# Deformable weights turned among the first products, and half an image out of PSUM before the second convolution: one fused network block on one core

## What is computed

```python
x = x + deformable(_gn(x))          # _gn: 32 groups of 4 channels
x = x + residual_block(_gn(x))

# deformable: om = conv3x3(x, w_off) gives 27 channels: 9 y-offsets, 9 x-offsets, 9 masks;
#   every tap samples x bilinearly at its own fractional position, times sigmoid(mask);
#   out = einsum(samples, weight) + bias, then a norm over 16 groups, gamma, beta
# residual_block: q = ternary(w) in {-1, 0, 1}
#   out1 = relu(batchnorm(conv3x3(x, q1)))
#   out2 = batchnorm(conv3x3(out1, q2));  return relu(out1 + out2)
```

## Time and profile before

| what | us |
|---|---|
| median of 3 runs (291.68 to 292.33) | 292.24 |
| the profiled execution, whole | 290.57 |
| its span, first to last instruction | 288.8 |
| TensorE busy | 251.1 |
| VectorE busy | 193.7 |
| ScalarE busy | 170.6 |
| GpSimd busy | 137.6 |

### The profile page before, as it was taken

How to read it: one execution, slowest core, us unless ns; L and a number is a source line. 1 busy time by engine, 2 the same in 40 slices (tenths; PEclk the granted TensorE clock), 3 DMA queues, 4 the chain that set the end, 5 groups by cost and what they waited for, 6 DMA issues and landing times.

```text
span 288.8 us, 5556 instructions
## 1 busy us (share of the span) xinstructions
PE 251.1 (87%) x1980; PEld 217.0 (75%) x1980; DVE 193.7 (67%) x450; ACT 170.6 (59%) x365; POOL 137.6 (48%) x193
## 2 busy tenths in 40 slices
PE   2699898999899899989989999999899949999900
PEld 2567567899898899989988889988687727777700
DVE  5588736989888996779977899770466253115194
ACT  2568646989669878878998778840143033330061
POOL 9202899967659688857769975140000000000040
PEclk9999997999999999999999999999999997999965
DMA  7915676543433323333323333000000000000016
GB/s 201 390 30 182 210 256 233 158 124 135 138 129 114 122 61 115 120 96 114 97 85 100 128 123 101 25 2 0 0 0 2 0 0 0 0 3 0 5 38 257
DMA packets 25737, 28.13 MB, mean 97 GB/s; under 512 B 2525, under 2 KB 23629, under 8 KB 25704
## 3 DMA queue, kind: packets, MB, share of 16 engines
q1 hardware_dynamic: 25200, 26.47, 28.1%
q10 hardware_dynamic: 504, 1.24, 1.2%
HBM read 19.87 MB, written 6.78 MB: 92 GB/s over the span
## 4 chain that ended last, share of the span: by engine, by line
PE 66%; DVE 16%; ACT 7%; DMA 4%; issue 2%; POOL 2%; SPq 1%; ACTq 0%; POOLq 0%
PE PS L787 25%; PE PS L707 6%; PE PS L660 5%; PE PS L708 5%; PE PS L709 5%; PE PS L689 4%; PE PS L691 4%; PE PS L690 4%; DVE slo L1298 4%; DMA wd_raw<-in_L_conv_weight 3%; ACT vhi L959 3%; PE PS L594 2%; DVE vlo L1309 2%; DVE xb L1401 2%; ACT shi L947 1%
## 5 line engine op out<-in xcount | busy, mean ns | idle before, releaser
L502 POOL TENSOR_TENSOR vt<-rowm,hat 128x1026 f32<-128x1026 f32 x36 | 70.8, 1968 | 28.4 <-PE PS L669 27.2
L1309 DVE TENSOR_TENSOR vlo<-PS,vhi 128x576 fp32r<-128x576 f32 (+2 forms) x88 | 50.0, 589 | 17.0 <-ACT vhi L959 16.7
L959 ACT ACTIVATE vhi<-PS 128x576 fp32r<-128x576 f32 (+2 forms) x88 | 43.8, 524 | 17.9 <-PE PS L691 17.8
L1298 DVE TENSOR_TENSOR slo<-PS,shi 114x512 fp32r<-114x512 f32 (+1 forms) x68 | 43.2, 675 | 8.9 <-ACT shi L947 8.6
L707 PE MATMUL PS<-vhi,wdhi 128*128 128x256 f32 x144 | 43.7, 304 | 1.8 <-ACT xb L966 1.8
L527 POOL TENSOR_TENSOR xb<-xb,xs 128x512 f32<-128x512 f32 x3 | 3.7, 1280 | 86.5 <-ACT xb L1031 86.5
L689 PE MATMUL PS<-shi,patch 114*128 114x288 f32 (+1 forms) x136 | 43.5, 320 | 0.3 <-DVE vlo L1309 0.2
L787 PE MATMUL PS<-xhi,q 128*128 128x512 f32 (+1 forms) x144 | 38.7, 415 | 4.2 <-ACT xhi L1026 4.2
L691 PE MATMUL PS<-shi,patch 114*128 114x288 f32 (+1 forms) x136 | 41.0, 301 | 0.0
L690 PE MATMUL PS<-slo,patch 114*128 114x288 f32 (+1 forms) x136 | 40.8, 300 | 0.0
L708 PE MATMUL PS<-vlo,wdhi 128*128 128x256 f32 x144 | 40.5, 281 | 0.0
(11 more groups left out here) (155 smaller groups left out, 429.6 us busy)
## 6 DMA issues: line engine op xcount, KB each, us to landing
patch<-xt SPq DMA_DIRECT2D x136, 114.0 KB
xt<-xtt SPq DMA_DIRECT2D x4, 1024.0 KB, 6.1
xs<-in_x SPq DMA_DIRECT2D x3, 512.0 KB, 8.6
out<-xb SPq DMA_DIRECT2D x6, 256.0 KB, 2.3
wraw<-in_L_conv_w SPq DMA_DIRECT2D x2, 576.0 KB, 10.8
wd_raw<-in_L_conv_weight ACTq DMA_DIRECT2D x1, 576.0 KB, 8.3
xs<-in_x SPq DMA_DIRECT2D x2, 256.0 KB, 3.7
omr<-omr SPq DMA_DIRECT2D x8, 64.0 KB, 3.8
```

Of the source, the lines that this page charges most:

```text
L502: g.tensor_tensor(vt[:, n % 2, :, :].rearrange("p t (r j) -> p t r j", r=WR), rowm[:, n % 2, :, :].unsqueeze(3).to_broadcast([P, TAPS, WR, ...
L959: last = a.activation(places(vhi), src, ACT.Copy)
L1298: d.tensor_tensor(lo, src, hi, ALU.subtract).then_inc(slo_ok, 1 if pairs(n) == 2 else 3)
L1309: last = d.tensor_tensor(places(vlo), src, places(vhi), ALU.subtract)
```

## The change

1. TensorE turns the deformable weights after the first six products, not before them, with `group_square` of image 1 between the second and third group of three; ScalarE writes `whole(GN0, 0)` ahead of the first copy of weights; VectorE's `deformable_lo(0)` goes behind the statistics of image 2.
2. GpSimd's low parts of image 2 go to VectorE (ahead of `whole_late(3)`), and VectorE's of image 3 to GpSimd, behind `distances(1)`. The four folds of the first ternary weight, which stood there, are spread over the rounds n = -1 to 1; those of the second go to n = 2 to 4.
3. Slot -1 on TensorE and ScalarE is ahead of the last three products of the offsets (3, 1) and of `tail(7)`.
4. In the first convolution the two tiny products of `GN8` of image 3 move behind the next quarter image each; VectorE takes the second half's statistics ahead of `variance(GN1, 2)`.
5. ScalarE copies PSUM bank 0 to `raw` (in `vt`, free by then) during the first convolution. Statistics, `r1` and `xhi` of half image 0 read `raw`; ScalarE writes `xhi` of half 0 first; the second convolution starts on it alone, and its seventh product waits for the second half.

```diff
+            FOLDED = {-1: ((0, 0),), 0: ((0, 1), (0, 2)), 1: ((0, 3),), 2: ((1, 0),), 3: ((1, 1),), 4: ((1, 2), (1, 3))}
...
                 if n == -4:
-                    for level in range(FOLDS):
-                        fold_weights(0, level)
-                if 0 <= n < FOLDS:
-                    fold_weights(1, n)
+                    low_parts(3)
+                for i, level in FOLDED.get(n, ()):
+                    fold_weights(i, level)
...
-            for part in range(2):
-                for h in range(2):
-                    offset_part(0, h, part)
+            offset_part(0, 0, 0)
+            for m in range(2):
+                turn_deformable(m)
+            group_square(GN0, 1)
+            turn_deformable(2)
+            offset_part(0, 1, 0)
+            for h in range(2):
+                offset_part(0, h, 1)
...
-                pe.wait_ge(ready, (B, 2)[part] + b + 1 if done is c1_mm else 2 * b + h + 1 + (h == 0))
+                if done is c1_mm:
+                    pe.wait_ge(ready, (B, 2)[part] + b + 1)
+                else:
+                    pe.wait_ge(ready, 2 * b + h + 1 + (h == 0 and (b, part) != (0, 0)))
                 for i, k in enumerate(TAP_ORDER[part]):
+                    if done is c2_mm and (b, h, part, k) == (0, 0, 0, 2 * K):
+
+                        pe.wait_ge(r1hi_ok, 2)
...
                 between = {(0, 0): [(group_mean, GN1, B - 2)],
-                           (0, 1): [(group_square, GN1, B - 2), (group_mean, GN8, B - 1)],
-                           (0, 2): [(group_square, GN8, B - 1)],
+                           (0, 1): [(group_square, GN1, B - 2)],
+                           (0, 2): [(group_mean, GN8, B - 1)],
+                           (1, 0): [(group_square, GN8, B - 1)],
...
+                            if (sums, n) == (group_mean, GN8):
+
+                                pe.wait_ge(gn_var, order(GN1, B - 2) + 1)
...
             turn_offsets(2)
-            offset_conv(3, 1)
+            offset_part(3, 1, 0)
             slot(-1)
+            offset_part(3, 1, 1)
...
+                act.wait_ge(c1_mm, 1)
+                act.wait_ge(vt_ok, CHUNKS)
+                a.activation(raw, PS[:, 0, :], ACT.Copy).then_inc(raw_ok, 1)
                 root(BN1, 0)
                 act.wait_ge(gn_ok, order(BN1, 0) + 1)
-                for n, hi in [(1, 1), (0, 1), (1, 0)] + [(n, hi) for n in range(2, 2 * B) for hi in (1, 0)]:
-                    if (n, hi) == (0, 1):
-                        act.wait_ge(r1_first, 1)
+                act.wait_ge(raw_ok, 1)
+                for n, hi in [(0, 1), (1, 1), (1, 0)] + [(n, hi) for n in range(2, 2 * B) for hi in (1, 0)]:
...
             heads(GN0, 0)
+            whole(GN0, 0)
             deformable_hi(0)
-            whole(GN0, 0)
...
-                variance(GN1, B - 2)
                 dve.wait_ge(y_done, 1)
                 image_stats(GN8, B - 1, halves=(1,))
+                variance(GN1, B - 2)
...
-                d.tensor_scalar(chunk(r1, 0), PS[:, 0, :], scale_of(BN1, 0), shift_of(BN1, 0), ALU.mult, ALU.add).then_inc(r1_first, 1)
+                d.tensor_scalar(chunk(r1, 0), raw, scale_of(BN1, 0), shift_of(BN1, 0), ALU.mult, ALU.add).then_inc(r1_first, 1)
...
             image_stats(GN0, 1)
-            deformable_lo(0)
             deviation(GN0, 1)
             dve.wait_ge(x_in[2], 16)
             image_stats(GN0, 2, last=False)
+            deformable_lo(0)
...
             pixels_lo(1)
+            tails(GN0, 2)
             whole_late(3)
             largest(0)
-            tails(GN0, 3)
```

More of the change, by code:

```diff
@@ L146, in build @@
         r1 = sb("r1", [P, B, HW])
+        raw = vt[:, 0, :, :].rearrange("p t q -> p (t q)")[:, 0:BIG]
         PS = ctx.enter_context(nc.psum_tensor("PS", [P, 2 * B, BIG], F32))
@@ L196, in build @@
         c1_mm, c2_mm = sem("c1_mm"), sem("c2_mm")
-        r1_first, r1_ok, r1hi_ok, r1lo_ok = (sem(n) for n in ("r1_first", "r1_ok", "r1hi_ok", "r1lo_ok"))
+        raw_ok, r1_first, r1_ok, r1hi_ok, r1lo_ok = (sem(n) for n in ("raw_ok", "r1_first", "r1_ok", "r1hi_ok", "r1lo_ok"))
         f_scaled, f_relu, out_done = (sem(n) for n in ("f_scaled", "f_relu", "out_done"))
@@ L472, in _ @@
             low_parts(0)
-            low_parts(2)
             def distances(n):
@@ L559, in _ @@
             group_square(GN0, 0)
-            for m in range(K):
-                turn_deformable(m)
             def turn_image(b):
@@ L1017, in finish @@
                 whole(GN1, B - 1)
+                act.wait_ge(c1_mm, 1)
+                act.wait_ge(vt_ok, CHUNKS)
+                a.activation(raw, PS[:, 0, :], ACT.Copy).then_inc(raw_ok, 1)
                 root(BN1, 0)
                 act.wait_ge(gn_ok, order(BN1, 0) + 1)
-                for n, hi in [(1, 1), (0, 1), (1, 0)] + [(n, hi) for n in range(2, 2 * B) for hi in (1, 0)]:
-                    if (n, hi) == (0, 1):
-                        act.wait_ge(r1_first, 1)
+                act.wait_ge(raw_ok, 1)
+                for n, hi in [(0, 1), (1, 1), (1, 0)] + [(n, hi) for n in range(2, 2 * B) for hi in (1, 0)]:
                     if hi and n // 2 >= RING:
                         act.wait_ge(c2_mm, 2 * (n // 2 - RING) + 2)
-                    dst, src, done = ((chunk(r1, n), PS[:, n, :], r1_ok), (chunk_rows(xhi, n), square(PS[:, n, :]), r1hi_ok))[hi]
+                    dst, src, done = ((chunk(r1, n), PS[:, n, :], r1_ok), (chunk_rows(xhi, n), square(PS[:, n, :] if n else raw), r1hi_ok))[hi]
                     a.activation(dst, src, ACT.Relu, bias=shift_of(BN1, 0), scale=scale_of(BN1, 0)).then_inc(done, 1)
@@ L1069, in _ @@
             slot(-2)
+            slot(-1)
             tail(7)
-            slot(-1)
             masks(2)
@@ L1215, in tails @@
                 dve.wait_ge(xhi_ok, (B if n == GN1 else 0) + b + 1)
-                dve.wait_ge(xn_late, b - 1) if (n, b) == (GN0, B - 1) else dve.wait_ge(xn_ok, (2 if n == GN1 else 0) + b + 1)
+                dve.wait_ge(xn_late, b - 1) if (n, b) == (GN0, 2) else dve.wait_ge(xn_ok, (2 if n == GN1 else 0) + b + 1)
                 d.tensor_tensor(inner(xlo, b), square(plain(b)), inner(xhi, b), ALU.subtract).then_inc(xlo_ok, 1)
@@ L1376, in conv_stats @@
                     for m in range(2 * B):
-                        dve.wait_ge(done, m + 1)
-                        ins = d.bn_stats(st[:, n, m, :], PS[:, m, :])
+                        dve.wait_ge(*((raw_ok, 1) if (n, m) == (BN1, 0) else (done, m + 1)))
+                        ins = d.bn_stats(st[:, n, m, :], raw if (n, m) == (BN1, 0) else PS[:, m, :])
                     link(ins)
```

10 lines of the change are left out of this document (5 added, 5 removed).

## The result

| | before | changed |
|---|---|---|
| median, us | 292.28 (291.68 to 294.35, 4 runs) | 288.59 (288.2 to 288.8, 4 runs) |
| the profiled execution, whole / span | 290.57 / 288.8 | 288.8 / 287.0 |

The ratio is 0.9895, 95% interval 0.9853 to 0.9938: faster by about 1%, and the median is inside the predicted range of 288.1 to 291.2. (Ratios in this document are estimates of their own, each with its interval; they are not the quotient of the two medians printed beside them.) Two differences don't agree, though: the medians are 3.7 us apart, the profiled executions 1.8. The forecast was 2.3.

A forecast was written before the change was run, and what follows sets the result against it. The prediction took TensorE, two thirds of the chain of waits, to bound the kernel. Its terms, -1.75 + 0.3 - 0.83 = -2.3 us, took the median from 292.24 to 289.9 us, range 288.1 to 291.2.

The forecast's parts named there:

- Weights among products: Opening: products start before the deformable weights are turned, bringing the replicating DMA earlier; -0.5 us, bounds 0 and -1.15.
- The rival that L1149 comes first: Opening: VectorE's small step runs ahead of GpSimd's subtraction, square 0.65 us earlier; 289.3 us, chance 0.13.
- GpSimd's folds, -1.1: Opening: one subtraction of 2.19 us replaces four folds of 3.27 ahead of the first `vt`; -1.1 us, bounds 0 and -1.1.
- Slot -1, -0.15: Slot -1: no wait for `tail(7)` first, pairs follow at once; -0.15 us, bounds +0.2 and -0.5.
- The opening together: Sum of the three opening terms, -0.5 - 1.1 - 0.15 = -1.75 us.
- First convolution, +0.3: First convolution: wait at the `GN8` mean reappears as 1.45 us at image 3's `GN1` mean; +0.3 us.
- rival bound -1.4: First convolution: lower bound, if the chain from square to aggregate is shorter by 1.4 us.
- Between the convolutions, -0.83: Between the convolutions: one ScalarE copy suffices before the second starts; -0.8 us, -0.83 in the sum, bounds -0.85 and -0.5.
- The rival that the clock holds here: Second convolution: the shorter TensorE wait of 3.4 us keeps the clock up, saving 1.6 us; 288.3 us, chance 0.10.
- From the sum to the median: Whole kernel: the gain of 2.3 us in the profiled execution is taken off the median 292.24, giving 289.9 us.
- The slower rival: First convolution: the new 1.45 us wait lets the clock fall, 291.5 us, or 293.1 with two lengths; slower, chance 0.04.

The follow-up runs named there:

- e7: Changed kernel with part 1 undone, the nine turned blocks ahead of the products again; 289.41 us, ratio 0.9891.
- e10: The kernel before, unedited, run once more for its trace; one execution, 295.93 us.
- e9: The kernel before with part 2 of the change alone; 290.76 us, ratio 0.998.
- e2: Changed kernel with parts 4 and 5 undone, only parts 1 to 3 kept; 288.96 us, ratio 0.9896.
- e3: Changed kernel with part 4 undone; 288.46 us, ratio 0.9887.
- e12: Changed kernel with `GN8` mean after a quarter's third product, GpSimd's first low parts after VectorE's deviation, image 3's low parts before `distances(0)`; 287.35 us, ratio 0.9865.
- e8: Changed kernel with GpSimd's low parts of image 0 waiting for VectorE's deviation of image 1; 288.54 us, ratio 0.9896.
- e6: Changed kernel with the four folds of the first ternary weight back ahead of the first `vt`; 294.47 us, ratio 1.0091.
- e5: Changed kernel with part 3 undone, last offset products and `tail(7)` ahead of slot -1 again; 289.27 us, ratio 0.9929.
- e1: The changed kernel again, no edit; 288.92 us, ratio 0.9907.
- e11: Changed kernel with `GN8` mean after a quarter's third product, square after that quarter, GpSimd's first low parts waiting for VectorE's deviation; 287.56 us, ratio 0.9866.

## Why the prediction was right, and where it was off

It was right in sign and range, and for the terms behind the opening nearly to the digit. By its steps:

- **Weights among products.** First product 10.28 (10.34 forecast), the held-up step to 14.25 (14.4), the square at 14.57 (14.47). Of the 0.5, the first distances show 0.31 (30.96 to 30.65), half of it the input's. What failed is the price of the turned blocks, 0.13 each: they ran at half speed, the six ahead of the square took 1.48 us and made it start 0.3 behind the end of L1167, and the three behind it took 0.68 instead of 0.4. More important, the term was sized for an execution whose wait was short. In e7 and e10 the old order stands 1.6 us before the square, and the next 13 products take 1.5 to 1.8 longer. The profile shown had 0.92 and lost nothing, so one trace couldn't price it. From `xhi` to image 1's first product of high parts (19.39 before, 19.08 changed) the old order takes 9.65, 9.95, 11.07 and 11.62 us (e9, before, e7, e10), the new one 9.37 to 10.45 in ten traces. The new order has no long wait, but it too can run at half speed until past 16 us (e2, e3, e12), so it narrows the loss and doesn't end it. The rival that L1149 comes first was priced wrong: with the step free in e8, the square comes no 0.65 earlier, because the turned blocks are ahead of it in the queue.
- **GpSimd's folds, -1.1.** `rowm` came at 34.17 instead of 35.59 (both by the timeline), 1.1 of it by this part; e6 shows 2.99 for the four folds at slot -2 and 5.6 in all.
- **Slot -1, -0.15.** The pairs of slot 0 come 46.03 - 44.45 = 1.58 us earlier, 0.17 more than slot -2 does: the forecast. But the pairs of slot 1 (50.30 instead of 51.72) are only 1.42 earlier, so it was given back in slot 0. The forecast had the turned offsets wait some 0.2 for `tail(7)`; they waited 0.31. Nothing of this term is seen at the first mean: from slot -2 on, both orders take the same time where their clock is alike (the stages above). The medians of e5 would allow 0.35 to 0.7, but its trace has 0.17 for the order.
- **The opening together**, -1.75 forecast, -1.35 at the first mean, the input's 0.15 included. This is the term that was too large in the trace. It hangs on the clock: e1's trace, with no half clock around slot 0, is 2.14 earlier than before's at the first mean.
- **First convolution, +0.3** (rival bound -1.4): 0.31, with the wait of 1.45 at the next mean measured as 1.34. A wait that is moved, not removed; e3 confirms it and e11 shows the way to remove it.
- **Between the convolutions, -0.83**: -0.81. The rival that the clock holds here did not come in this trace: nine products took 3.32, half clock, after 3.40 us of waiting. It does come: in e7 the clock held over the same 3.40 us, and the last stage was 1.5 us shorter, near the 1.6 that the rival was priced at. So its ground against it, that no wait nearly as long had left the clock up, was too weak.
- **From the sum to the median.** The step "I take the same difference from the median" failed. In the trace the gain was 1.8, in the medians 3.7 and then 2.0 (e1). Executions of the changed kernel spread less: 287.1 to 290.0 over 16, against 288.8 to 295.0 over 62 of before, 14 of them over 293. A gain in the frequency of long executions isn't in any single trace. What makes them rarer isn't shown. Mean granted clock rose from 0.960 to 0.968, but that alone doesn't do it: e9 has 0.967 and no gain, e10 is long at 0.968.
- **The slower rival**, a fall of the clock in the new wait: none in any of the seven traces that have it.

What stays open: how often the old order runs into the long wait, how much of before's spread is a late image (seen once, in e10) and how much half clock. There are two traces of before, one short and one long; the timed runs record only span and mean clock. And since e9's trace and its median disagree by 1.9 us, the shares of parts 1 and 2 in the gain are known only for executions like the profiled ones.

## What to carry to other kernels

A wait that is moved to another tiny product comes back behind the chain it sits in; ask how long that chain is and by how many products its start was moved, and move it by the fewest that cover the wait (three here, not nine). Price a stall of TensorE together with the work behind it: in two traces here a stall of 1.6 us was followed by 13 products that lost another 1.5 to 1.8 us, so work that can lie in such a stall may be worth more than its own time. Before a difference between two traces is put down to an edit, see where each had its half clock: in e5 it made 1.48 of 1.65 us. When timed runs of a kernel spread by more than the gain in question, cut several traces at the same points and compare stage by stage: two stages here repeated to 0.06 us, while the medians moved by half a microsecond.

## What the runs showed of the hardware

- A 128x1 step of VectorE that reads two operands from SBUF took 0.22 us alone (e8) and 1.13, 1.51, 1.86, 1.90 and 2.23 when GpSimd's subtraction of 2.2 us ran beside it, ending with it each time (before and changed, e7, e9, e10).
- The products behind a wait of 1.57 and 1.64 us ran at half speed for the next 13 or nearly (e10, e7); behind waits of 0.85 and 0.92, at the same place, they did not (e9, before). The wait isn't shown to be the cause: in e10 the products ahead of it were slow already, and without any wait the new order ran at half speed until past 16 us in e2, e3 and e12. In the first convolution waits of 1.16 and 1.34 behind long busy stretches did nothing.
- The granted-clock column can read 1.00 where matrix products take twice their time (e10, 19 to 21 us; six products in 2 us). So it does in the opening of the other traces: in the changed kernel it is 1.00 from 10.28 on, where three products take 1.57. Durations of a known product are the safer reading.
- A wait alone doesn't tell whether the clock falls. It held over 3.40 us between the convolutions in e7 and fell over the same wait in eight other traces. It fell at about 39 us in e5, where TensorE's longest wait in the 5 us before was 0.43.
- The same program's first input landed 3.27 us later in one execution (e10) than in another.
